# A vision tower on one Trainium2 core: the last group's experts summed in SBUF, and another order for row sums, image statistics and factors

## The chip, the cores and the metric

The kernel runs on one core of one Trainium2 chip, as one program. A core has TensorE (PE, matrix products), VectorE (DVE), ScalarE (ACT), GpSimd (POOL) and SyncE (SP, which here only issues transfers), each with its own instruction stream; they meet at semaphores. The metric is the time of one execution on the device in microseconds (us). The profile is of one other execution; its times are counted from the start of its span.

## What is computed

64 images of 2 x 104 x 104 become 128 channels by 170 tokens each (169 patches of 8 x 8 and a class token). There is one layer, in three stages:

```python
# token stage: the image and four diagonal shifts of it by 4 pixels, one layernorm per image, a patch convolution
concat = jnp.concatenate((x, lu, ru, ld, rd), axis=1)
mean = jnp.mean(concat, axis=(1, 2, 3), keepdims=True); var = jnp.var(concat, axis=(1, 2, 3), keepdims=True)
normed = (concat - mean) * jax.lax.rsqrt(var + EPS) * gamma[None] + beta[None]
y = conv(normed, W, stride 8) + b ; h = concat([cls_tok, tokens])
# graph stage: layernorm over channels, a two-layer graph convolution over the 128 channels, a projection
h = h + graph(_layernorm(h))
# attention and experts: causal attention in 2 heads with normalised q and k, then 8 experts, all of them for every token
gate = softmax(y @ gate_W + gate_b)
hid = gelu(einsum('bnd,edf->bnef', y, W1) + b1)
eo = einsum('bnef,efd->bned', hid, W2) + b2
h = h + einsum('bned,bne->bnd', eo, gate)
```

The mean and variance of an image need sums over all its pixels, of which the four shifted copies lose a rim.

## The kernel before

**Tiling.** The result tile `ht` is 128 channels by 64 x 170 tokens, f32. The expert layer works on groups of 4 images (`T` = 680 columns, halves of `TH` = 340, 16 groups). Each group's 8 experts have 4 chunks of 128 hidden rows each, in all 32 slots. In slot s PE forms hidden rows s (`of_o`, L1059), ScalarE applies the gelu (L667, and for most slots a half-precision copy, L672), DVE forms the difference part (L1537) and for eight slots the copy (L1535), and three slots later PE multiplies both with the second weights (`experts_out`, L1094). After every fourth slot DVE's `weigh` (L1550) takes the two halves of an expert's sum out of PSUM, adds the bias and multiplies by the gate row, into one of two `tmp` tiles. GpSimd adds that tile to the output in DRAM by an accumulating transfer (L498), eight per group, each after the one before it has landed; SP has stored the group's base, `ht` without the experts, by a plain transfer (L405). The gate rows go to a scratch in DRAM and come back spread over the partitions in three transfers (L398).

**Preamble.** The token stage runs over 65 points (13 rows of patches by 5 shifts). At each, DVE multiplies a row by gamma (`gammas`, L1347) and PE convolves (L816). Beside the points an order written out by hand says what else each engine does at which point: for the first group its graph stage and queries and keys (`GRAPH_0`, `QK_0`), for the second its first layernorm (`FIRST_1`), the folding of the first weights with the attention's output matrix (`FOLD_PE` products L783, `FOLD_HI` copies on ScalarE, `FOLD_LO` differences on DVE, `first_lo`, L1463), and 20 further points (`LATE`, 65 to 84) with no convolution. `kn` (L1420) scales the keys and waits for PE's cast of the roots (L857).

**Image statistics.** Images 0 to 7 are summed at the start. For images 8 to 63 accumulating transfers add rows into `sums4` while the token stage runs. `sums_rest` (L1277 to L1295, three parts) reduces these on DVE, at points 62, 63 and 64 in `DVE_SUMS`; `image_stats` (L825) is one product on PE; `image_moments` (L1302 to L1306) and `image_factors` (L1313 to L1325, twelve dependent operations of 128x56) are on DVE. The factors are first used by `fix` (L1371, L1374) from slot 6 of the first group's expert stage on.

**First attention.** After the late points DVE takes the row maxima of the scores in two parts (L1428, L1431), ScalarE the exponentials (L633), DVE normalises (L1436, L1443), PE turns the probabilities (L995) and weighs the values (L1007). In between PE does products of the second group's graph stage (L829) into another PSUM pair. The scores of part 1 use the PSUM pair in which the folds and the statistics' product are.

## Time and profile before

| | us |
|---|---|
| timed runs, median (lowest to highest) | 1461.5 (1458.69 to 1461.71) |
| profiled execution, own time | 1459.82 |
| its span | 1457.8 |
| PE busy | 1415.5 (97%) |
| DVE busy | 1215.5 (83%) |
| ScalarE busy | 1106.4 (76%) |
| GpSimd busy | 290.9 (20%) |

A timeline row gives the start, the length, the engine, the line, the operation with tiles and shapes, how many of them, and in brackets how long the engine was idle in front and what released it. Rows of several instructions can overlap a little with the next one, so the distance between two starts is the better price. Most tiles are parts of one SBUF tensor and appear as `area`; `pair` is PSUM. The granted TensorE clock (PEclk) is a share of 2.4 GHz: 1.00 is 2.4 GHz, 0.50 is 1.2 GHz.

### The profile page before, as it was taken

The page shows a single profiled execution, that of the slowest core. Times are in us where ns is not written, and L with a number is a line of the kernel's source. Part 1 is how long each engine was busy: PE and PEld are TensorE (multiplying, and loading weights), DVE is VectorE, ACT ScalarE, POOL GpSimd, SP SyncE. Part 2 cuts the span into 40 slices and gives each one's busy share as a digit, 9 for nine tenths or more (in the row PEclk, how much of TensorE's full clock was granted, in tenths as well). Part 3 has the DMA queues.
Part 4 walks back from the last instruction along what each step waited for, and adds up shares of the span by engine and source line. Part 5 has one row for each costly group of instructions (what it writes and reads, how often), then busy time and mean ns, then how long its engine had stood idle before and what let it go on. Part 6 is the DMA issues. An engine that isn't in the chain of part 4 may idle for free.

```text
span 1457.8 us, 31164 instructions
## 1 busy us (share of the span) xinstructions
PE 1415.5 (97%) x10945; PEld 982.8 (67%) x10945; DVE 1215.5 (83%) x2576; ACT 1106.4 (76%) x1880; POOL 290.9 (20%) x293
## 2 busy tenths in 40 slices
PE   8998899999999999999999999999999999999997
PEld 5665667676676677676676677676676767676665
DVE  7886898888888888889788888889888888887765
ACT  5343678787878888887878878888878878878766
POOL 2124032131301212131301212131301112130101
PEclk9999999999999999999999999999999999999999
DMA  8796232434333332424233332424342332424334
GB/s 263 180 237 128 105 61 30 121 43 109 45 107 46 80 73 29 124 38 114 39 108 45 93 60 29 124 38 115 40 113 38 100 53 33 120 38 116 49 99 57
DMA packets 40771, 125.54 MB, mean 86 GB/s; under 512 B 5792, under 2 KB 6048, under 8 KB 38560
## 3 DMA queue, kind: packets, MB, share of 16 engines
q0 software_dynamic: 22464, 55.81, 26.3%
q1 hardware_dynamic: 18128, 69.28, 13.2%
q8 instruction: 19, 0.31, 0.1%
q14 instruction: 16, 0.13, 0.0%
q10 hardware_dynamic: 144, 0.01, 0.0%
HBM read 68.98 MB, written 50.48 MB: 82 GB/s over the span
## 4 chain that ended last, share of the span: by engine, by line
PE 74%; DVE 10%; DMA 7%; issue 5%; ACT 2%; DVEq 0%; POOL 0%; SPq 0%; POOLq 0%; ACTq 0%
PE pair L1094 25%; PE pair L1059 22%; PE pair L829 9%; PE pair L816 4%; DMA area<-gate_scratch 3%; DVE area L1537 3%; PE pair L1007 3%; PE pair L924 2%; PE pair L980 2%; PE pair L995 2%; DMA area<-area 2%; PE pair L955 1%; DVE area L1550 1%; DMA gate_scratch<-gt_t 1%; ACT area L672 1%
## 5 line engine op out<-in xcount | busy, mean ns | idle before, releaser
L667 ACT ACTIVATE area<-pair,pack_b_sb 128x680 f32<-128x680 f32 x512 | 423.5, 827 | 180.6 <-PE pair L1059 180.5
L1537 DVE TENSOR_TENSOR area<-area 128x680 f16<-128x680 f32 x512 | 454.0, 892 | 110.1 <-ACT area L672 104.1
L1059 PE MATMUL pair<-area,ws 128*128 128x340 f16 x3072 | 530.7, 308 | 5.5 <-ACT area L667 2.8
L1094 PE MATMUL pair<-area,ws 128*128 128x340 f16 x3072 | 526.8, 307 | 6.9 <-DVE area L1550 3.8
L1094 PEld LDWEIGHTS pair<-area,ws 128*128 128x128 f16 x3072 | 290.2, 98 | 160.6 <-DVE area L1550 26.4
L1059 PEld LDWEIGHTS pair<-area,ws 128*128 128x128 f16 x3072 | 292.4, 97 | 155.0 <-ACT area L667 8.3
L672 ACT ACTIVATE area<-pair,pack_b_sb 128x680 f16<-128x680 f32 x384 | 316.2, 824 | 0.0
L498 POOL DMA_DIRECT2D tower_out<-area x128 | 114.2, 892 | 997.3 <-DVE area L1550 943.4
L1550 DVE SCALAR_TENSOR_TENSOR area<-pair,pack_b_sb,area 128x340 f32<-128x340 f32 x256 | 133.9, 565 | 10.2 <-PE pair L1094 8.5
L633 ACT ACTIVATE area<-pair,nbias,root 85x85 f32<-85x85 f32 (+1 forms) x256 | 112.5, 466 | 0.2
L455 POOL TENSOR_TENSOR area<-area 128x680 f16<-128x680 f32 x56 | 89.2, 1601 | 45.3 <-ACT area L596 43.0
L596 ACT ACTIVATE area<-pair,pack_b_sb 128x680 f32<-128x680 f32 x92 | 81.9, 936 | 4.4 <-PE pair L829 3.8
L1535 DVE CAST area<-area 128x680 f16<-128x680 f32 x128 | 67.0, 524 | 12.2 <-ACT area L667 5.7
L816 PE MATMUL pair<-area,pack_a_sb 128*128 128x336 f32 (+1 forms) x164 | 56.1, 484 | 4.4 <-DVE area L1347 3.5
L1443 DVE TENSOR_SCALAR area<-area,rs 85x85 f32<-85x85 f32 (+1 forms) x256 | 56.4, 281 | 2.3
L633 ACT ACTIVATION_READ_ACCUMULATOR area<-pair,nbias,root 85x1 f32 x256 | 54.9, 214 | 0.0
L641 ACT ACTIVATE area<-pair,att_b 128x340 f16<-128x340 f32 x32 | 17.3, 540 | 40.7 <-PE pair L1007 40.7
L816 PEld LDWEIGHTS pair<-area,pack_a_sb 128*128 128x128 f32 x164 | 30.9, 195 | 24.5 <-DVE area L1347 5.6
L571 ACT ACTIVATE ht<-pair 128x392 f32<-128x392 f32 (+1 forms) x26 | 19.8, 871 | 34.9 <-PE pair L816 34.9
L1450 DVE COPY area<-pair 85x510 f32<-85x510 f32 x64 | 43.4, 678 | 2.3 <-PE pair L995 0.4
L995 PE MATMUL pair<-ident,area 85*85 85x85 f32 x384 | 41.9, 246 | 3.1 <-DVE area L1467 2.4
L924 PEld LDWEIGHTS pair<-head_m,area 128*85 128x85 f32 x512 | 43.5, 156 | 1.9
(238 smaller groups left out, 1758.5 us busy)
## 6 DMA issues: line engine op xcount, KB each, us to landing
tower_out<-area POOLq DMA_DIRECT2D x128, 340.0 KB, 4.7
area<-gate_scratch SPq DMA_DIRECT2D x16, 1360.0 KB, 9.9
area<-gate_scratch SPq DMA_DIRECT2D x16, 1020.0 KB, 7.1
area<-cells SPq DMA_DIRECT2D x16, 392.0 KB, 8.7
area<-cells POOLq DMA_DIRECT2D x14, 392.0 KB, 6.5
area<-area POOLq DMA_DIRECT2D x14, 392.0 KB, 6.3
tower_out<-ht SPq DMA_DIRECT2D x16, 340.0 KB, 2.3
area<-gate_scratch SPq DMA_DIRECT2D x16, 340.0 KB, 4.4
```

The lines of the kernel that those rows point to most:

```text
L455: pool.tensor_tensor(h1_l[:, half], relu[c], h1_h[:, half], ALU.subtract).then_inc(relu_lo, 1)
L498: pool.dma_start(out[:, g * T:(g + 1) * T], tmp[e % 2], accum_op=ALU.add).then_inc(out_done, 16)
L596: last = nc.scalar.activation(two(part), halves(ps), ACT.Relu, bias=scal[:, 4 + c:5 + c], scale=scal[:, c:c + 1])
L633: nc.scalar.activation(probs[:, b * SCORE + o0:b * SCORE + o0 + w], score_ps_at(b)[:, h, c * QC:c * QC + w], ACT.Exp, bias=nbias[:, n:n + ...
L667: nc.scalar.activation(two(hid[slot % NHID]), halves(hid_ps[slot % 2]), ACT.Gelu_apprx_tanh, bias=col(COL_B1 + slot)).then_inc(hid_ready, 1)
L672: nc.scalar.activation(two(hh[slot % NPART]), halves(hid_ps[slot % 2]), ACT.Gelu_apprx_tanh, bias=col(COL_B1 + slot)).then_inc(hhi_act, 1)
L816: last = mm(cells_ps(p, j), conv_w[:, shift * D:(shift + 1) * D], xg[n % XG][:, c0 * BZ:c1 * BZ], start=(shift == 0), stop=(shift == SHIFT ...
L829: last = mm(ps[:, j, 0:TH], lhs, rhs[:, j, :], start=start, stop=stop)
L1059: last = mm(hid_ps[slot % 2][:, j, 0:TH], lhs[:, w], rhs[:, j * TH:(j + 1) * TH], start=(i == 0), stop=(i == 2))
L1094: last = mm(eo_ps[:, j, 0:TH], lhs[:, w], rhs[:, j * TH:(j + 1) * TH], start=(m % CH == 0 and i == 0), stop=(m % CH == CH - 1 and i == 2))
L1537: v.tensor_tensor(hl[slot % NPART], hid[slot % NHID], hh[slot % NPART], ALU.subtract).then_inc(hlo_ready, 1)
L1550: v.scalar_tensor_tensor(tmp[e % 2][:, j * TH:(j + 1) * TH], eo_ps[:, j, 0:TH], b2_s[:, e:e + 1], gbc[:, e * T + j * TH:e * T + (j + 1) * ...
```

## The change

Three things. In the last group there is no base store and no accumulating transfer: DVE's `weigh` adds each weighted half to `ht` in SBUF, and SP stores the two halves when the eighth expert has been added. The row sums move behind the last gamma, to points 66 to 68, and `kn` and three of the fold's differences move forward. The statistics' product goes behind the scores of the first attention, into the second half of the pair `eo_ps`; the moments go between the two parts of the maxima, and the factors behind the second part, out of slot 4 of the first expert stage.

```diff
-        "cast": 62, "kn": 73}
+        "cast": 62, "kn": 65}
-DVE_SUMS = {62: 0, 63: 1, 64: 2}
+DVE_SUMS = {66: 0, 67: 1, 68: 2}
-IMG_SLOT = 4
-FOLD_LO = {0: 36, 1: 36, 2: 42, 3: 46, 4: 64, 5: 69, 6: 77, 7: 77}
+FOLD_LO = {0: 36, 1: 36, 2: 42, 3: 46, 4: 64, 5: 65, 6: 69, 7: 70}
...
+            def last_store():
+                for j in range(2):
+                    half = slice((G - 1) * T + j * TH, (G - 1) * T + (j + 1) * TH)
+                    sp.wait_ge(part_added, 2 * (E - 1) + j + 1)
+                    sp.dma_start(out[:, half], ht[:, half]).then_inc(last_out, 16)
             for g in range(G):
-                base(g)
+                if g < G - 1:
+                    base(g)
...
-            for g in range(G):
+            for g in range(G - 1):
                 weigh(g, later=g > 0, ahead=g < G - 2)      # GpSimd
...
-                if b == 0 and not later:
-                    pe.wait_ge(tok_done, 2 * NP)
+                if b == 2 and not later:
+                    pe.wait_ge(img_step[1], 3)              # PE, values
...
                 elif m == 1:
-                    pe.wait_ge(img_step[1], 3)
+                    pe.wait_ge(fold_lo, E)                  # PE, scores
...
                     for m in range(NB // 2):
                         scores(g, m, later)
+                    pe.wait_ge(tok_done, 2 * NP)
+                    image_stats(1, BZ, eo_ps[:, 1, 0:2 * BZ])
...
-            pe.wait_ge(fold_lo, E)
-            image_stats(1, BZ, hid_ps[1][:, 1, 0:2 * BZ])
...
-                    for m in range(NB // 2):
-                        maxima(g, m)
+                    maxima(g, 0)
+                    image_moments(1, BZ, eo_ps[:, 1, 0:2 * BZ])
+                    maxima(g, 1)
+                    image_factors(1, BZ, BA)
...
-                if e >= 2 or later:
+                if (e >= 2 or later) and not (last and e >= 2):
                     dve.wait_ge(out_done, 16 * (g * E + e - 1))
...
+                if last:
+                    for j, done in enumerate((half_ready, tmp_ready)):
+                        dve.wait_ge(done, g * E + e + 1)
+                        if e:
+                            dve.wait_ge(part_added, 2 * (e - 1) + j + 1)
+                        acc = ht[:, g * T + j * TH:g * T + (j + 1) * TH]
+                        v.tensor_tensor(acc, acc, tmp[e % 2][:, j * TH:(j + 1) * TH], ALU.add).then_inc(part_added, 1)
...
-                    if not later and slot == IMG_SLOT:
-                        image_factors(1, BZ, BA)
```

## Rows read from the trace of the kernel before

**Rows 1.** Timeline of DVE, 130 to 151 us, its rows explained above.

```profile
132.73 0.39 DVE L1277 TENSOR_TENSOR statz<-area 128x224 f32<-128x224 f32 x1 [9.27 <-DMA area<-area]
...
134.86 0.91 DVE L1347 TENSOR_TENSOR area<-area,pack_a_sb 128x728 f32<-128x728 f32 x1
135.69 0.85 DVE L1283 TENSOR_TENSOR area<-area 128x672 f32<-128x672 f32 x1
...
137.61 0.91 DVE L1347 TENSOR_TENSOR area<-area,pack_a_sb 128x728 f32<-128x728 f32 x1
...
139.04 0.27 DVE L1291 SCALAR_TENSOR_TENSOR statz<-statz 128x112 f32<-128x112 f32 x1
...
139.84 0.68 DVE L1463 TENSOR_TENSOR ws<-pair,ws 128x512 f16<-128x512 f32 x1
140.44 0.85 DVE L1420 TENSOR_TENSOR area<-area,pair 128x680 f32<-128x680 f32 x1
...
144.02 0.22 DVE L1302 COPY statz<-pair 128x56 f32<-128x56 f32 x1 [0.57 <-PE pair L825]
...
145.49 1.28 DVE L1428 TENSOR_REDUCE mx<-pair 85x4 f32<-85x340 f32 x2 [0.75 <-PE pair L984]
...
146.95 1.28 DVE L1428 TENSOR_REDUCE mx<-pair 85x4 f32<-85x340 f32 x2
...
150.25 0.17 DVE L1436 RECIPROCAL rs<-sm 85x4 f32<-85x4 f32 x1 [1.82 <-ACT area L633]
```

**Rows 2.** Timeline of PE, 131 to 146 us.

```profile
131.58 0.75 PE L857 MATMUL pair<-ident,area 85*128 85x85 f32 x8
135.83 4.55 PE L816 MATMUL pair<-area,pack_a_sb 128*128 128x392 f32 x8 [3.50 <-DVE area L1347]
...
145.38 1.12 PE L980 MATMUL pair<-area 64*85 64x85 f32 x16
```

**Rows 3.** Timeline of all engines, 169 to 198 us.

```profile
169.87 1.29 SPq L398 DMA_DIRECT2D area<-gate_scratch  x3
...
172.14 0.18 DVE L1313 TENSOR_SCALAR statz<-statz 128x56 f32<-128x56 f32 x1
...
175.10 0.92 DVE L1407 SCALAR_TENSOR_TENSOR area<-area,pack_b_sb,pair 128x680 f32<-128x680 f32 x1
...
177.53 1.32 PE L829 MATMUL pair<-area,wqk_h 128*128 128x340 f16 x4 [3.00 <-DVE area L1413]
...
178.17 1.04 DVE L1550 SCALAR_TENSOR_TENSOR area<-pair,pack_b_sb,area 128x340 f32<-128x340 f32 x2
...
197.87 1.08 PE L1094 MATMUL pair<-area,ws 128*128 128x340 f16 x6 [0.96 <-DVE area L1550]
```

**Rows 4.** Windows between gate reductions: length, each engine's busy time, PEclk, DMA share, GB/s.

```profile
162.76:249.33 86.57, 82.14 (x664) 57.40 (x663) 77.37 (x163) 66.33 (x113) 25.73 (x23) 0.98 0.37 82
249.33:331.07 81.74, 80.89 (x664) 56.77 (x663) 69.97 (x151) 66.31 (x113) 16.59 (x15) 1.00 0.35 73
```

The busy times stand in the order PE, PE's weight loads, DVE, ScalarE, GpSimd.

**Rows 5.** Windows around two falls of the granted clock, same columns.

```profile
1378.50:1381.80 3.30, 1.51 (x19) 1.26 (x17) 3.26 (x11) 3.30 (x16) 0.54 (x1) 0.98 0.72 93
1381.80:1392.00 10.20, 9.94 (x68) 7.34 (x68) 4.95 (x16) 3.79 (x10) 0.00 (x0) 0.50 0.03 6
...
177.50:180.30 2.80, 2.77 (x11) 1.52 (x12) 2.79 (x5) 0.85 (x2) 0.79 (x1) 0.52 0.95 399
```

**Rows 6.** Window in the last group's expert stage, same columns.

```profile
1411.00:1446.00 35.00, 35.00 (x245) 23.54 (x244) 24.55 (x36) 27.70 (x37) 4.63 (x5) 1.00 0.38 51
```

**Rows 7.** The end: timeline, SP's final wait, and the page's transfers (KB, us to landing).

```profile
1449.77 1.05 DVE L1550 SCALAR_TENSOR_TENSOR area<-pair,pack_b_sb,area 128x340 f32<-128x340 f32 x2 [0.70 <-PE pair L1094]
...
L414 SPq EVENT_SEMAPHORE  x1: 17/17/17, 1456.9 to 1456.9; - x1
...
tower_out<-area POOLq DMA_DIRECT2D x128, 340.0 KB, 4.7
...
tower_out<-ht SPq DMA_DIRECT2D x16, 340.0 KB, 2.3
area<-gate_scratch SPq DMA_DIRECT2D x16, 340.0 KB, 4.4
```

More of the change, by code:

```diff
@@ L297, in vit_tower @@
         half_used, half_ready, base_done, out_done = map(sem, ("half_used", "half_ready", "base_done", "out_done"))
+        part_added, last_out = map(sem, ("part_added", "last_out"))
         PREP_PE, PREP_ACT, PREP_DVE = 9, 8, 22
@@ L412, in _ @@
                         second_weights(e)
-            sp.wait_ge(base_done, 16 * G)
-            sp.wait_ge(out_done, 16 * E * G)
+            last_store()
+            sp.wait_ge(base_done, 16 * (G - 1))
+            sp.wait_ge(out_done, 16 * E * (G - 1))
+            sp.wait_ge(last_out, 32)
         @block.gpsimd
@@ L1537, in experts, with weigh @@
                 v.tensor_tensor(hl[slot % NPART], hid[slot % NHID], hh[slot % NPART], ALU.subtract).then_inc(hlo_ready, 1)
-            def weigh(g, e, later):
+            def weigh(g, e, later, last=False):
                 dve.wait_ge(half_used, g * E + e + 1)
@@ L1551, in weigh, with expert_slot @@
                                            gbc[:, e * T + j * TH:e * T + (j + 1) * TH], ALU.add, ALU.mult).then_inc(done, 1)
-            def expert_slot(g, slot, later):
+                if last:
[5 more added lines that the diff above has]
+                        v.tensor_tensor(acc, acc, tmp[e % 2][:, j * TH:(j + 1) * TH], ALU.add).then_inc(part_added, 1)
+            def expert_slot(g, slot, later, last=False):
                 if slot >= LAG and (slot - LAG) % CH == CH - 1:
-                    weigh(g, (slot - LAG) // CH, later)
+                    weigh(g, (slot - LAG) // CH, later, last)
                 if slot < SLOTS:
@@ L1562, in ffn @@
                 for slot in range(SLOTS + LAG):
-                    expert_slot(g, slot, later)
-                    if not later and slot == IMG_SLOT:
-                        image_factors(1, BZ, BA)
+                    expert_slot(g, slot, later, last=not successor)
                     if successor and 0 <= slot - SLOTS < NB // 2:
@@ L1603, in _ @@
                     prepare(DVE_PREP[n])
+            for n in LATE:
                 if n in DVE_SUMS:
                     sums_rest(DVE_SUMS[n])
-            for n in LATE:
                 chain(n)
-            image_moments(1, BZ, hid_ps[1][:, 1, 0:2 * BZ])
             attention(0, False, True)
```

## The prediction

> **What bounds the kernel now.** I read the waits of 100 to 200 us first, because three of the four edits lie there, then the timelines of VectorE (DVE) and TensorE (PE) through that stretch, then windows over one pass of the experts' loop, and last the final 35 us. The kernel is one long preamble (token stage, first group's attention), then 15 more groups that repeat, then a tail.
>
> In the preamble the reader should see one hole. At point 62 of the token stage DVE stands at the image row sums, which wait for the accumulating transfers: idle 9.27 us, until 132.73 [rows 1]. Two multiplications by gamma (points 63 and 64, L1347 at 134.86 and 137.61) are behind it on DVE, so PE, which starts the cast of the roots at 131.58 and is through at 132.3, idles 3.50 us and ends its last convolutions at 140.4 [rows 1, 2]. After that DVE is the engine that everything follows, until it starts the first normalisation at 150.25, which waited 1.82 us for ScalarE's exponentials; these waited for the maxima (1.28 for a pair of reductions at 145.49 and at 146.95) [rows 1].
>
> In the first group's expert stage DVE has no gap from 168 on. The image factors (L1313 to L1325) stand in it from 172.14 to 175.10; behind them is the chain xh, its half-precision parts, which PE awaits for 3.00 us before the queries at 177.53 [rows 3]. The first such pass, from one gate reduction to the next, takes 86.57 us, a later one 81.74 with PE busy for 80.89 of it: later groups are bound by PE, and the diff touches none of them but the last [rows 4].
>
> At the end PE has finished and the time is a transfer: the last two products (L1550) end at 1450.82, the accumulating store takes 4.7 us from its issue and lands at 1456.9, 0.9 before the span's end [rows 7]. It is issued only at about 1452.2 (1456.9 - 4.7), since it waits for its predecessor.
>
> **Part A, row sums and moments.** After the change gammas 63 and 64 run at 123.5, when DVE used to go idle. PE's order is unchanged, it is busy until 132.3, and then both convolutions are ready. They end at least the 3.50 us of that wait earlier, and as the second also stood for its gamma (137.61 + 0.91), near 134.8 in place of 140.4: 5.6 is the upper bound of this part. But DVE now sets the pace. From 132.3 it does: kn (L1420, moved from 73 to 65), 0.8, and first_lo 5, 0.6 (start to start 139.84 to 140.44), to 133.7; here the sums start 1.0 later than before. Row sums part 0 without the gamma, 132.73 to 134.86, 2.1; part 1, 135.69 to 137.61, 1.9; part 2, 139.04 to 139.84, 0.8; first_lo 6 and 7, 1.2: DVE is at 139.8. The second scores now wait for fold_lo, so the first maxima, 139.8 to 141.2 (1.46 from one pair to the next), run beside the second scores, which take no longer than that; the statistics' product and its latency 0.6 (the wait at 144.02), moments, three operations at 0.25 (the twelve of the factors took 2.96), 0.7: 142.5; second maxima 1.4, 143.9; factors 2.96, 146.9. ScalarE has had its first bias since 141.2; before, it took 3.3 us from the bias (146.95) to the first normalisation (150.25), table load included, so it is ready at 144.5 and has 2.4 in hand: no wait remains there [rows 1, 3]. Normalise starts at 146.9 against 150.25: 3.4 us. From there both versions run the same DVE list. Ends: -1.0 (sums later, nothing else gained) and 5.6; I take 3.4, the sum of DVE's own rows.
>
> What is behind the added waits: PE now holds scores 1 for fold_lo, and behind it plain, values and the second group's graph products. By the same sums (my estimates) it idles 2.0 us, from 137.8 to 139.8, and again about 2.3, from 146.2 to 148.5, when the first values are copied out. The work there has slack, as DVE is late, if the clock holds (below). ScalarE is free of it.
>
> **Part B, factors out of the expert stage.** They took 175.10 - 172.14 = 2.96 us of a DVE without gaps, and PE's 3.00 us wait ends with the same chain [rows 3]. With them gone hx's parts end at 174.5, just as PE arrives. The granted clock after the old wait was 0.52 for 2.8 us [rows 5], so PE also saves up to 1.4 there; but PE meets DVE again at 197.87 (a wait of 0.96 for L1550), where only DVE's gain counts. Late next would be the gate row for the first expert: issued at 169.87, 4.4 to land, 174.3, while DVE needs it at 178.17 - 2.96 = 175.2 [rows 3, 7]. It stays hidden by 0.9. Ends: 2.1 (that transfer late by twice its margin) and 4.83 (86.57 - 81.74, the whole excess of the first pass) [rows 4]; I take 3.0.
>
> **Part C, last group.** Removed: one plain store of the base (hidden at 1331.8), 8 accumulating stores on GpSimd, waits for them. Added on DVE: 16 additions of 128x340 f32. A tensor_tensor of 672 columns took 0.85 and one of 224 took 0.39 [rows 1], so 340 take 0.51, 0.43 from start to start. All but the last two lie beside PE's work. In 35 us of that group, five experts, DVE is busy 24.55 and PE 35.00 [rows 6]: an expert leaves DVE 2.1 us free, its two additions take 0.9. Queued behind them is the next difference part (L1537), which PE needs only three slots later. So I cost them at nothing; were that cover gone, the sixteen would cost 6.9. The last two are on the path: 1450.8 + 0.43 + 0.51 = 1451.75. The first half's store is issued at 1451.4, the second's at 1451.8. A plain store of 340 KB took 2.3 us to land [rows 7]; a half has no row and lies between 1.2 (half of that) and 2.3 plus 1 for the other half in its way. I take 2.1, near the whole one, as both are in flight together. Landing 1453.9 against 1456.9: 3.0. Ends: 1.8 and 3.9.
>
> The Trainium skill speaks against splitting the store: its page "DMA: Bandwidth & Descriptors", section "Anatomy of one DMA — SWDGE (gpsimd) path", puts about 2.0 us of fixed cost on each transfer and only the bytes over 436 GB/s on top, and its rules advise coalescing. By it the last half takes 2.4 and one whole store behind the second addition 2.8, so the split would still save 0.4, and part C would be 2.7. The trace is below that formula: a whole store of 340 KB took 2.3, not 2.8 [rows 7]; no run here shows a half.
>
> **Sum.** 3.4 + 3.0 + 3.0 = 9.4. The profiled execution took 1459.8 (span 1457.8): 1450.4. The median of the three timed runs is 1461.5, 1.7 above it, which would give 1452.1; I name 1451.0, between the two. The ends of all three parts together would be 1456.9 and 1445.5; I don't expect them at once.
>
> **Rivals.**
> 1. The clock falls in the first attention. In the last group's attention PE was busy 1.51 of 3.30 us, and then the granted clock was 0.50 (1.2 GHz) for 10.2 us; after the 3.00 us wait before 177.53 it was 0.52 for 2.8 us [rows 3, 5]. The new waits of 2.0 and 2.3 us are between those cases. If it falls at 148.5, graph 2, two turns and two weighings and graph 3 double: some 4.5 us more, less 0.7 of slack: about 4, time 1455. 20%.
> 2. More returns in the first expert stage: PE's gain of 4.4 isn't stopped at 197.87 because the splits on GpSimd meet DVE at another place. 1.4 more: 1449.6. 12%.
> 3. The additions are not hidden: with 32 waits of DVE on itself and its own lateness, difference parts come late and PE waits 6.9 in the last group: 1457.9, no measurable change. Against it: the slack above. 4%.
> 4. Slower than before: the clock falls already at 137.8 and stays down through all of the first attention, which is nearly continuous PE work from the second scores at 145.4 to the gate reduction at 162.76 (17.4 us) [rows 2, 4]. At 1.2 GHz that is up to 17.4 more, less 4.3 of waits that it fills: 13, time 1464. It decides from 9.4 us of path work at the lower clock. For it: the 10.2 us row. Against: here products of 340 columns stand between the small ones, and behind such work the clock was back after 2.8 us. 3%.
> 5. The reordering of A gains nothing because another wait, not seen, holds DVE at the old time: 1454.4. 5%.
> The forecast has the rest, 56%.
>
> **Numbers.** About 0.2% (2.9 us) is what a measurement of this kernel can tell from no change. The range 1447.5 to 1455.8 holds the forecast with its ends, rival 2, 5 and most of 1. Faster by more than 0.2% are the forecast and rivals 1, 2 and 5, 93%; a little of that I leave for the spread of the runs. Slower is rival 4; rival 3 and the spread are no change.
>
> **What would show it.** Right: L1347's last two before 126, L1277 at about 133.6 with a wait only on PE's cast in front, L816 ending near 135, L1436 first at 147; L1407 right behind L1537 at slot 4 with no PE wait over 0.5 before the queries; a pass of 83 to 84 us; 16 DVE additions in the last group with PE still 35 of 35 busy; the last landing 3 us behind the last product. Wrong: a granted clock of 0.5 between 137 and 160; PE waits for L1537 after 1404; a half store of 3 us or more.

## The result, and the profile after

| | before | after |
|---|---|---|
| timed runs, median (lowest to highest) | 1461.71 (1458.69 to 1463.63), 5 runs | 1451.83 (1449.51 to 1456.65), 5 runs |
| profiled execution, own time | 1459.82 | 1456.65 |
| its span | 1457.8 | 1454.9 |

The ratio is 0.9937 (95% interval 0.9918 to 0.9955): 9.9 us less by the medians, where 10.5 was forecast against 1461.5. The profiled execution of after is the slowest of its five; it shows the first rival at work.

Line numbers after the insertions are up to 13 higher: gamma is L1356, `conv` L825, the row sums L1286 on, the moments L1311 on, the factors L1322 to L1334, the maxima L1437, normalise L1445, the difference part L1548, `weigh` L1561, the new additions L1569, the last stores L411.

The timeline of DVE, 120 to 152 us, answers to [rows 1]:

```profile
123.78 5.58 DVE L1356 TENSOR_TENSOR area<-area,pack_a_sb 128x728 f32<-128x728 f32 x4
...
134.42 0.86 DVE L1429 TENSOR_TENSOR area<-area,pair 128x680 f32<-128x680 f32 x1 [3.80 <-PE pair L866]
...
135.80 0.38 DVE L1286 TENSOR_TENSOR statz<-area 128x224 f32<-128x224 f32 x1
...
142.10 1.27 DVE L1437 TENSOR_REDUCE mx<-pair 85x4 f32<-85x340 f32 x2
...
144.02 0.22 DVE L1311 COPY statz<-pair 128x56 f32<-128x56 f32 x1 [0.45 <-PE pair L834]
...
148.73 0.22 DVE L1334 SCALAR_TENSOR_TENSOR img<-statz,img 128x56 f32<-128x56 f32 x1
148.99 0.17 DVE L1445 RECIPROCAL rs<-sm 85x4 f32<-85x4 f32 x1
```

The wait for the accumulating transfers is gone; DVE waits for PE's cast instead. The gammas are through when it comes, the sums stand behind `kn`, and from 134.42 to the first normalisation DVE has one wait of 0.45. The last four gammas took 5.58 us, 1.4 each, where two took 1.73 in the kernel before; GpSimd was at work on the folds beside them from 124.96 to 131. They end at 129.36, or 127.3 in before's time, where the forecast wanted them before 126; in front of a wait of 3.80 that costs nothing. That GpSimd slows them is likely (its cast beside them took 1.83, one of the same shape at 131.01 without them 0.61), but no run tests it. PE in the same stretch [rows 2]:

```profile
133.63 0.75 PE L866 MATMUL pair<-ident,area 85*128 85x85 f32 x8
134.22 2.65 PE L825 MATMUL pair<-area,pack_a_sb 128*128 128x392 f32 x8
...
142.24 1.12 PE L989 MATMUL pair<-area 64*85 64x85 f32 x16 [2.19 <-DVE ws L1472]
...
147.17 1.36 PE L838 MATMUL pair<-area,gcn_m 128*128 128x340 f32 x4
150.81 0.66 PE L1004 MATMUL pair<-ident,area 85*85 85x85 f32 x6 [2.27 <-DVE area L1476]
```

The last eight convolution products take 2.65 without a wait, where they had 3.50 of wait and 4.55. So the old wait had a fall of the clock behind it too: the granted clock was 0.59 from 136 to 140 in before's trace and is 1.00 there in after's. The two new waits are there, 2.19 and 2.27. Windows, with the columns of [rows 4]: first the stretch behind the second wait, then the first pass of the experts from gate reduction to gate reduction, then the window of [rows 6], moved by nothing:

```profile
152.00:163.00 11.00, 11.00 (x65) 8.32 (x63) 6.21 (x17) 2.10 (x4) 0.00 (x0) 0.50 0.00 1
167.28:250.78 83.50, 81.08 (x664) 56.77 (x663) 74.99 (x152) 66.28 (x113) 25.88 (x23) 1.00 0.37 85
1411.00:1446.00 35.00, 35.00 (x245) 23.59 (x243) 28.24 (x46) 27.63 (x36) 0.00 (x0) 1.00 0.00 1
```

The granted clock is 0.50 (1.2 GHz) for all of 152 to 163: PE is busy without a gap and gets half as much done. The pass is 83.50 against 86.57. In the last group PE is full and GpSimd empty, and DVE has 3.7 more in 35 us. PE in the first pass, and the end (timeline, the DMA view, SP's final wait), answer to [rows 3, 7]:

```profile
199.31 1.08 PE L1105 MATMUL pair<-area,ws 128*128 128x340 f16 x6 [1.71 <-DVE area L1561]
```

```profile
1450.55 1.05 DVE L1561 SCALAR_TENSOR_TENSOR area<-pair,pack_b_sb,area 128x340 f32<-128x340 f32 x2 [0.70 <-PE pair L1105]
1451.51 0.93 DVE L1569 TENSOR_TENSOR ht<-ht,area 128x340 f32<-128x340 f32 x2
1452.04 0.81 SPq L411 DMA_DIRECT2D tower_out<-ht  x2
...
tower_out<-ht SPq DMA_DIRECT2D x2, 170.0 KB, 1.9
...
SPq L423 <- DMA tower_out<-ht: 1.5, 1, 1.5
```

From the end of the last `weigh` (1450.55 + 1.05 = 1451.60) to the end of the span are 3.30; before they were 6.98 (1457.8 - 1450.82).

**Where the 2.9 us between the two profiled executions went.** I cut both traces at the same events and compare the pieces; with this table the experiments are read too. The columns: A, from the start of PE's cast of the roots to the first normalisation; att, from there to the first gate reduction; B, from the first gate reduction to the second; last, from the 16th gate reduction to the last `weigh`'s end; C, from there to the span's end; conv, the start of PE's next products behind the first convolution's 32 products, near 20 us. The stretch between the second and the 16th gate reduction is left out. Clock is the mean granted clock of the whole execution.

| kernel | conv | A | att | B | last | C | span | clock |
|---|---|---|---|---|---|---|---|---|
| before | 20.30 | 18.67 | 12.51 | 86.57 | 58.45 | 6.98 | 1457.8 | 0.993 |
| after | 22.36 | 15.36 | 18.29 | 83.50 | 58.05 | 3.30 | 1454.9 | 0.991 |
| again | 22.35 | 16.75 | 13.73 | 83.51 | 58.05 | 3.26 | 1451.4 | 0.993 |
| fill | 24.40 | 17.02 | 12.34 | 83.11 | 58.05 | 3.3 | 1452.2 | 0.995 |
| graph2 | 22.12 | 15.36 | 13.96 | 83.51 | 58.10 | 3.2 | 1450.0 | 0.995 |
| late | 20.84 | 13.80 | 16.32 | 86.14 | 58.09 | 3.25 | 1451.5 | 0.993 |
| fill2 | 22.30 | 15.35 | 12.34 | 83.89 | 57.60 | 3.3 | 1448.9 | 0.995 |
| tail | 20.43 | 18.94 | 12.51 | 86.96 | 58.57 | 3.28 | 1454.5 | 0.994 |
| sums62 | 23.84 | 21.21 | 12.34 | 83.56 | 58.06 | 3.26 | 1455.2 | 0.995 |
| adds2_whole | 22.46 | 15.35 | 13.67 | 83.62 | 58.99 | 3.60 | 1450.8 | 0.995 |
| slot4 | 21.90 | 13.22 | 12.50 | 87.35 | 58.07 | 3.2 | 1449.9 | 0.995 |
| fill_last | 22.32 | 15.36 | 12.35 | 83.90 | 58.38 | 3.26 | 1446.6 | 0.998 |
| fill_all | 21.66 | 15.36 | 12.35 | 82.77 | 58.60 | 3.22 | 1445.8 | 1.000 |

Before to after: A -3.31, B -3.07, C -3.68, together -10.06. Against that stand +2.06 before 22 us, where the diff changes nothing, and +5.78 in the first attention; both are stretches at a lower granted clock. The rest is -0.3 in the middle and -0.4 in the last group.

### The profile page after: what moved, and what is told of

It is laid out like the page before. It is cut to its first block, busy times and chain, and to the rows that moved or that the text cites. A ratio compares the mean times of both kernels' runs of the same rounds, so it can differ in the third digit from the quotient of the medians.

```text
span 1454.9 us, 31173 instructions
## 1 busy us (share of the span) xinstructions
PE 1419.2 (98%) x10945; PEld 986.4 (68%) x10945; DVE 1223.4 (84%) x2592; ACT 1105.7 (76%) x1880; POOL 284.9 (20%) x285
## 4 chain that ended last, share of the span: by engine, by line
PE 75%; DVE 12%; issue 6%; DMA 5%; ACT 2%; DVEq 0%; SPq 0%; ACTq 0%; POOLq 0%
PE pair L1105 25%; PE pair L1070 22%; PE pair L838 9%; PE pair L825 4%; DVE area L1548 3%; PE pair L1016 3%; DMA area<-gate_scratch 2%; PE pair L1004 2%; PE pair L933 2%; PE pair L989 2%; DVE area L1561 1%; DMA area<-area 1%; PE pair L964 1%; ACT area L681 1%; DMA gate_scratch<-gt_t 1%
## 5 line engine op out<-in xcount | busy, mean ns | idle before, releaser
L1548 DVE TENSOR_TENSOR area<-area 128x680 f16<-128x680 f32 x512 | 454.1, 892 | 104.9 <-ACT area L681 99.1
L507 POOL DMA_DIRECT2D tower_out<-area x120 | 106.8, 890 | 925.3 <-DVE area L1561 909.5
L1561 DVE SCALAR_TENSOR_TENSOR area<-pair,pack_b_sb,area 128x340 f32<-128x340 f32 x256 | 133.9, 565 | 9.8 <-PE pair L1105 8.6
L825 PE MATMUL pair<-area,pack_a_sb 128*128 128x336 f32 (+1 forms) x164 | 54.2, 473 | 0.9 <-ACT ht L580 0.9
L1004 PEld LDWEIGHTS pair<-ident,area 85*85 85x85 f32 x384 | 39.4, 163 | 11.6 <-DVE area L1452 8.1
L825 PEld LDWEIGHTS pair<-area,pack_a_sb 128*128 128x128 f32 x164 | 30.3, 190 | 19.6 <-issue 2.0
```

The costliest lines, as they stand in the source:

```text
L507: pool.dma_start(out[:, g * T:(g + 1) * T], tmp[e % 2], accum_op=ALU.add).then_inc(out_done, 16)
L825: last = mm(cells_ps(p, j), conv_w[:, shift * D:(shift + 1) * D], xg[n % XG][:, c0 * BZ:c1 * BZ], start=(shift == 0), stop=(shift == SHIFT ...
L1004: last = tr(eo_ps[0:QC, b % 2, n * QC:(n + 1) * QC], probs[:, b * SCORE + n * QC:b * SCORE + (n + 1) * QC], ident[0:QC, 0:QC])
L1548: v.tensor_tensor(hl[slot % NPART], hid[slot % NHID], hh[slot % NPART], ALU.subtract).then_inc(hlo_ready, 1)
L1561: v.scalar_tensor_tensor(tmp[e % 2][:, j * TH:(j + 1) * TH], eo_ps[:, j, 0:TH], b2_s[:, e:e + 1], gbc[:, e * T + j * TH:e * T + (j + 1) * ...
```

## The experiments

The theory: the three parts bring what their terms say, and what an execution of the changed kernel loses again is the granted clock, which falls behind PE's new waits in some executions. The rival for the 5.78: a new wait of PE or DVE that costs time by itself. Each part has a test of its own besides.

### again: the changed kernel once more

No edit.

> The changed kernel unaltered, five more times. Theory C (clock): its times fall into two kinds. Where the granted clock does not fall in the first attention 1449 to 1452; where it falls after the 2.3 us wait in front of the first turn of probabilities, 1455 to 1457, and then the span has a mean clock lower by about 0.003 or more. Rival W (order): the first attention is longer because of the new waits themselves, in every execution, and the times scatter around 1452 without two kinds.

1451.85 (1449.55 to 1456.11, 6 runs), ratio 0.9937 (0.9921 to 0.9953). The parts repeat to 0.04 us in B and C. The clock doesn't. Windows of this execution:

```profile
138.00:142.00 4.00, 1.83 (x19) 0.98 (x18) 3.83 (x10) 0.74 (x2) 0.00 (x0) 0.99 0.00 0
142.00:146.00 4.00, 3.98 (x27) 3.07 (x28) 2.06 (x7) 2.54 (x7) 0.00 (x0) 0.59 0.02 4
146.00:150.00 4.00, 3.84 (x34) 2.65 (x32) 3.59 (x15) 4.00 (x21) 0.00 (x0) 1.00 0.00 0
150.00:154.00 4.00, 2.02 (x9) 1.59 (x10) 3.90 (x15) 3.34 (x12) 0.00 (x0) 0.77 0.00 0
154.00:158.00 4.00, 4.00 (x32) 3.05 (x31) 2.97 (x13) 0.23 (x1) 0.00 (x0) 0.81 0.00 0
158.00:162.00 4.00, 4.00 (x41) 3.17 (x40) 2.75 (x5) 0.86 (x2) 0.00 (x0) 1.00 0.01 2
```

It fell twice, once behind each new wait (2.19 at 142.02, 2.15 at 151.98), each time for some 3 to 4 us: A is 1.39 longer than after's and att 1.39 longer than the 12.34 of undisturbed executions. In the profile of after it fell behind the second wait alone, and for 13 us. So one kernel has several courses through this stretch: A and att together took 33.65 in after's trace and 30.48 in this one, against 27.69 with both waits filled (fill2, below).

The two kinds of times that were expected did not come: the six spread over the whole range. Nor does the mean clock put them in order. 1456.11 has a mean clock of 0.994, as 1452.19 has, and among the five runs of after 1455.39 has 0.994, as 1451.83 has. The fall accounts for the 5.78 of the profiled execution (0.991), but these two slow ones are some 4 us above others of the same clock. The kernel before has such executions too (1465.83 and 1459.58, both at 0.993). What makes them is open; no trace was taken of one.

### fill: products in the second wait

26 products of 128x170 in half precision, into a part of PSUM that nobody reads until it is overwritten, ahead of the first turn. The output is unchanged.

```diff
+                if not later:
+                    for _ in range(26):
+                        mm(fr_ps[:, 0, TH:TH + 170], wv_h[:, :], xh_h[:, 0:170], start=False, stop=False)
```

> 26 extra products of 128x170 f16 (some 1.9 us of TensorE work whose result nobody reads) stand in the wait in front of the first turn of probabilities. Theory C: the granted clock stays at 1.00 from 150 to 163 us, the first attention is as short as forecast (first normalisation to gate reduction about 12.5 us, against 18.3 in the profile of the changed kernel), all five times are 1449 to 1452. Rival W: the extra work sits in front of the turns and helps nothing: normalisation to gate reduction stays near 18, times 1452 to 1457.

1450.98 (1448.66 to 1453.96, 5 runs), ratio 0.9924 (0.991 to 0.9938). The second wait is filled, the clock stays at 1.00 behind it, and att is 12.34. The times reach beyond the 1449 to 1452 that were expected: the profiled execution is the slowest of the five, with 2.0 more than after's in conv and 1.66 more in A. The first wait stayed open, and in this execution it cost:

```profile
144.41 1.94 PE L989 MATMUL pair<-area 64*85 64x85 f32 x16 [2.52 <-DVE ws L1475]
```

Sixteen products that take 1.12 at full clock took 1.94, and DVE then waited 1.77 for the statistics' product behind them. That is the part of the theory I had not priced: the first wait has its own fall, worth 1.4 to 1.7 in A.

### graph2: useful work in the second wait

The second group's graph product 2 is issued ahead of the first turn, not behind it.

```diff
+                if not later:
+                    graph_of(2)
...
-                graph_of(2)
+                if later:
+                    graph_of(2)
```

> The second group's graph product 2 moves in front of the first turn of probabilities in the first attention, so the wait there shrinks from 2.3 to about 1.1 us with no work added. Theory C: no fall of the clock, normalisation to gate reduction about 12.5 us or 0.3 less, times 1449 to 1451. Rival W: no change from the changed kernel.

1452.69 (1450.23 to 1454.22, 5 runs), ratio 0.9941 (0.9926 to 0.9955): no gain. The wait of 2.3 became three shorter ones, and the clock fell behind the third:

```profile
150.59 0.66 PE L1004 MATMUL pair<-ident,area 85*85 85x85 f32 x6 [1.14 <-DVE area L1479]
152.18 0.66 PE L1004 MATMUL pair<-ident,area 85*85 85x85 f32 x6 [0.93 <-DVE area L1479]
153.67 0.68 PE L1004 MATMUL pair<-ident,area 85*85 85x85 f32 x6 [0.25 <-DVE area L1455]
...
154.00:158.00 4.00, 4.00 (x21) 2.74 (x20) 2.27 (x8) 0.54 (x1) 0.00 (x0) 0.58 0.01 2
```

The work borrowed from between the turns filled one hole by opening others. What held the clock in these runs was extra products (fill2) or the wait gone (slot4).

### late: the factors behind the second part of the first attention's output

```diff
-                    image_factors(1, BZ, BA)
...
+                if not later:
+                    image_factors(1, BZ, BA)
```

> The factors (2.96 us on VectorE) move from in front of the first normalisation to behind the second o_lo of the first attention, in front of dev2. Theory C: normalisation starts 2.4 us earlier, when ScalarE is ready, TensorE's wait in front of the first turn is near 0, no fall of the clock; 2.0 of the 2.4 are given back before dev2, where VectorE idled 0.95: about 0.4 faster than a changed kernel without the fall, 1449 to 1451. Rival W: the factors are as costly there, the times stay as in the changed kernel, 1452 to 1456.

1452.90 (1449.0 to 1457.57, 6 runs), ratio 0.9944 (0.9925 to 0.9962): not better. Normalise came 1.56 earlier than after's (13.80 against 15.36), although the clock had fallen in front of it. But att is 3.98 above the undisturbed 12.34, and B is 2.6 above after's. 2.96 of the first is the factors again, now in front of the gate reduction; the other 1.0 includes the end of the first fall (the clock is 0.72 from 146 to 148) and was not taken apart:

```profile
158.31 0.18 DVE L1322 TENSOR_SCALAR statz<-statz 128x56 f32<-128x56 f32 x1
...
161.46 0.86 DVE L1410 TENSOR_TENSOR area<-ht,pair 128x680 f32<-128x680 f32 x1 [0.24 <-DVE img L1334]
```

The second is the clock: PE now waits behind them, 1.48 for the gate stage's ScalarE row (it is busy for 1.53 of the 3.00 us from 160 to 163), and the granted clock is 0.50 from 165 to 171.

```profile
163.18 1.57 PE L850 MATMUL pair<-mean_m,area 128*85 128x1 f32 x16 [1.48 <-ACT area L612]
...
165.00:167.00 2.00, 1.94 (x7) 1.04 (x8) 1.86 (x6) 1.61 (x5) 0.00 (x0) 0.50 0.00 0
167.00:169.00 2.00, 2.00 (x8) 0.90 (x6) 0.07 (x1) 1.52 (x2) 0.00 (x0) 0.50 0.00 0
```

The factors' 2.96 are on the path in both places, and each place opens a hole of PE's of its own.

### fill2: both new waits filled

Fill's products, and 26 of the same ahead of the second scores.

```diff
+                        if m == 0:
+                            for i in range(26):
+                                mm(fr_ps[:, 0, TH:TH + 170], wv_h[:, :], xh_h[:, 0:170], start=(i == 0), stop=(i == 25))
```

> The changed kernel with products that nobody reads (26 of 128x170 f16, some 1.9 us) in both waits of TensorE in the first attention: between the scores of part 0 and part 1, and in front of the first turn. Theory C (the waits let the clock fall, now in the one, now in the other): clock 1.00 from 133 to 166 us, cast of the roots to first normalisation 15.4 us, from there to the gate reduction 12.4, median 1 to 3 us below the changed kernel's 1451.8, with only the scatter of the first 20 us left (up to 4 us). Rival W (the clock is set by something other than these waits): falls as in the changed kernel, the same median.

1450.45 (1449.46 to 1450.83, 5 runs), ratio 0.9918 (0.9905 to 0.9931). The clock is 1.00 from 134 to 162:

```profile
142.18 1.12 PE L989 MATMUL pair<-area 64*85 64x85 f32 x16 [0.28 <-DVE ws L1478]
...
150.76 0.66 PE L1004 MATMUL pair<-ident,area 85*85 85x85 f32 x6 [0.37 <-DVE area L1482]
```

A is 15.35 and att 12.34. Both releasers are as late as before the filling (142.18 against 142.24, 150.76 against 150.81), so the waits by themselves cost nothing; this rules the rival out. The runs also lie closer, with a standard deviation of 0.48 us against 2.14 in again. That is five runs against six, and fill_last, below, has the same fillings and 2.12, by one execution of 1452.69; so the closer times are no proof that the fillings remove the spread. The median is 1.4 lower; the intervals of the two ratios overlap, so the gain on the median is likely and not shown, while the loss in single executions (5.8 in after's) is shown in the traces.

### tail: part C alone on the kernel before

The last group's additions and stores, and nothing of the order of sums, moments and factors. The lines shown are the additions; the base store and the accumulating transfers of the last group go too, as in the change.

```diff
+                if last:
+                    for j, done in enumerate((half_ready, tmp_ready)):
+                        dve.wait_ge(done, g * E + e + 1)
+                        if e:
+                            dve.wait_ge(part_added, 2 * (e - 1) + j + 1)
+                        acc = ht[:, g * T + j * TH:g * T + (j + 1) * TH]
+                        v.tensor_tensor(acc, acc, tmp[e % 2][:, j * TH:(j + 1) * TH], ALU.add).then_inc(part_added, 1)
```

> Only part C on the kernel before: the last group's experts summed in SBUF, two plain stores. Theory: everything up to the last weighing as before, from the gate reduction of the last group to the last weighing 58.1 to 58.5 us, last weighing to the end of the span 3.3 in place of 7.0: 3.7 faster, 1457.5 against 1461.2. Rival (additions on the path): 58.45 grows by several us and the gain is under 1.

1458.38 (1455.21 to 1460.88, 12 runs), ratio 0.9973 (0.9964 to 0.9982), 3.6 below before's 1461.97 of the same session. C is 3.28 against 6.98, so 3.70; A, att and B are before's within 0.4. Part C stands alone and is worth about 3.7.

### sums62: the row sums back at points 62 to 64

Row sums ahead of the last gammas again; the rest of the change kept.

```diff
-DVE_SUMS = {66: 0, 67: 1, 68: 2}
+DVE_SUMS = {62: 0, 63: 1, 64: 2}
```

> The changed kernel with the row sums back at points 62 to 64, in front of the last two gammas; all else as changed. Theory: VectorE idles again some 9 us for the accumulating transfers, TensorE 3.5 in front of the last convolutions; both gammas (1.7) and their convolutions and the folds behind them come after, so the first normalisation is 2 to 4 us later than in the changed kernel (cast of the roots to normalisation 17.5 to 19.5 against 15.4). Rival: the row sums were not the bound there, within 1 us of the changed kernel.

1455.04 (1451.8 to 1457.01, 6 runs), ratio 0.9946 (0.9933 to 0.996): 3.2 above the changed kernel by the medians, 4.6 above fill2. PE's wait for the gamma is back, and the second gamma with it:

```profile
139.78 2.04 PE L825 MATMUL pair<-area,pack_a_sb 128*128 128x392 f32 x4 [3.92 <-DVE area L1356]
142.53 2.79 PE L825 MATMUL pair<-area,pack_a_sb 128*128 128x392 f32 x4 [0.71 <-DVE area L1356]
```

and DVE waits for the folds, as these wait for PE:

```profile
147.69 0.69 DVE L1472 TENSOR_TENSOR ws<-pair,ws 128x512 f16<-128x512 f32 x1 [2.45 <-ACT ws L656]
...
149.65 1.28 DVE L1437 TENSOR_REDUCE mx<-pair 85x4 f32<-85x340 f32 x2
```

A is 21.21 against 15.36, 5.85 longer, where 2 to 4 were expected (17.5 to 19.5). The rest is the clock: PE was at 0.50 from about 140.6 to 147.4, the four products of 142.53 took 2.79 in place of 1.3, and the four of the folds behind them 3.03 in place of 1.88. The first two of the folds are what DVE's wait of 2.45 ends with, so the clock makes up some 2.3 of the 5.85 (my estimate from these rows), and 3.5 are left for the order. Against before, A is 2.54 longer: 1.90 behind the first maxima, where factors and moments now stand (6.66 against 4.76 [rows 1]), and 0.64 in front of them. In A and B together sums62 is only 0.47 below before, and after 6.38. So the new order of the row sums is what pays for the factors' new place.

### adds2_whole: twice the additions, one whole store

For the first seven experts of the last group each addition is done twice (the second into a tile that nobody reads), and the group is stored by one transfer behind the last addition. DVE also waits for each expert's spare additions before the next expert's.

```diff
-                for j in range(2):
-                    half = slice((G - 1) * T + j * TH, (G - 1) * T + (j + 1) * TH)
-                    sp.wait_ge(part_added, 2 * (E - 1) + j + 1)
-                    sp.dma_start(out[:, half], ht[:, half]).then_inc(last_out, 16)
+                whole = slice((G - 1) * T, G * T)
+                sp.wait_ge(part_added, 2 * E)
+                sp.dma_start(out[:, whole], ht[:, whole]).then_inc(last_out, 16)
...
+                    if e < E - 1:
+                        for j in range(2):
+                            v.tensor_tensor(xh[:, j * TH:(j + 1) * TH], dev[:, j * TH:(j + 1) * TH],
+                                            tmp[e % 2][:, j * TH:(j + 1) * TH], ALU.add).then_inc(spare, 1)
```

> Two edits in the last group, each with its own interval in the trace. (1) For experts 0 to 6 each addition is done twice, the second into a scratch tile: 1.7 us of VectorE per expert against a free 2.1. Theory: hidden, gate reduction to last weighing stays 58.1 (within 0.3). Rival: already the change's additions ate the cover, then it grows by up to 6. (2) One store of 340 KB behind both additions in place of two halves: lands 0.3 to 0.5 later than the second half did, last weighing to end of the span 3.7 against 3.3; by the Trainium skill's formula (2.0 us plus bytes over 436 GB/s, page DMA: Bandwidth & Descriptors) 0.4 later.

1452.59, one run. The window of [rows 6] and the one wait of PE in it:

```profile
1411.00:1446.00 35.00, 34.23 (x238) 22.84 (x237) 31.79 (x55) 26.50 (x34) 0.00 (x0) 1.00 0.00 1
...
1444.64 1.91 PE L1104 MATMUL pair<-area,ws 128*128 128x340 f16 x12 [0.77 <-DVE area L1547]
```

DVE is busy 31.79 of 35 and PE loses 0.77 once; last grows by 0.94. The fourteen more additions are 6.5 us of DVE time and cost 0.94. The wait is more than the 0.3 that was expected, far less than the rival's 6. So the sixteen of the change are hidden, with room for nearly as many again. The whole store ends 0.30 later than the two halves (3.60 against 3.30).

### slot4: part A without the factors in front of the normalisation

Fill2's first filling, the factors back in slot 4 of the first expert stage.

```diff
-                    image_factors(1, BZ, BA)
...
+                    if not later and slot == 4:
+                        image_factors(1, BZ, BA)
```

> As the kernel with both waits filled (1450.5), but the factors back in slot 4 of the first expert stage, and the second filling left out, since that wait goes with them. It prices the move of the factors by itself, with the clock held in the first attention. Theory: normalisation starts as soon as ScalarE is ready (13.0 us after the cast of the roots, not 15.4), and the first pass of the experts takes 86.5 in place of 83.5 to 83.9, with TensorE's 3 us wait and the clock at half behind it: net 0.6 slower, about 1451. Rival (parts A and B add up as forecast, 3 us for the factors): 3 slower, 1453.5.

1451.71 (1450.84 to 1452.46, 5 runs), ratio 0.9929 (0.9917 to 0.9942). Normalise is 2.13 earlier than fill2's and now waits for ScalarE; the wait before the queries is back at its old size:

```profile
146.01 0.17 DVE L1450 RECIPROCAL rs<-sm 85x4 f32<-85x4 f32 x1 [0.73 <-ACT area L642]
...
173.28 0.76 PE L838 MATMUL pair<-area,wqk_h 128*128 128x340 f16 x4 [3.00 <-DVE area L1427]
```

B is 87.35 against 83.89: 2.13 gained, 3.46 lost. Moving the factors is worth 1.3 us by itself, by the pieces (A and B together 100.57 against 99.24) and by the medians (1451.71 - 1450.45), though the intervals of these two overlap. The two terms A and B of the forecast are not independent: without the factors in it A is 5.45 (18.67 - 13.22), and B then nothing (87.35 against before's 86.57).

### fill_last: the clock of the last attention held

Fill2, and 43 such products at five places of the last group's attention, where the clock fell in the kernel before [rows 5].

```diff
+                def spare(n):
+                    if not ahead:
+                        for _ in range(n):
+                            mm(fr_ps[:, 0, TH:TH + 170], wv_h[:, :], xh_h[:, 0:170], start=True, stop=True)
```

> As the kernel with both waits filled (1450.5), and 43 more such products in the waits of the last group's attention, where TensorE runs at half clock for some 10 us in every profile so far. Theory C: the clock stays at 1.00 there, from the last maxima to the gate reduction about 17.5 us in place of 20.9, 1447.1 by the median. Rival: VectorE sets the pace of that attention anyway, under 1 us.

1447.65 (1446.18 to 1452.69, 6 runs), ratio 0.9907 (0.9892 to 0.9922), 2.8 below fill2; the intervals of the two overlap a little, so it is the traces that show the gain. A window of 20 us over that attention, first before, then fill_last (where the attention ends at 1384.96 and the experts' stage follows); and the last maxima and the gate reduction in fill2 and in fill_last:

```profile
1376.00:1396.00 20.00, 16.26 (x128) 11.67 (x126) 14.00 (x43) 12.97 (x42) 0.93 (x1) 0.74 0.13 18
```

```profile
1376.00:1396.00 20.00, 18.26 (x172) 13.08 (x169) 14.13 (x36) 14.91 (x30) 0.00 (x0) 1.00 0.21 43
```

```profile
1371.03 1.28 DVE L1443 TENSOR_REDUCE mx<-pair 85x4 f32<-85x340 f32 x2 [0.84 <-PE pair L993]
1388.03 0.29 DVE L1509 TENSOR_REDUCE lg<-pair 85x64 f32<-85x128 f32 x1 [1.74 <-PE pair L1069]
```

```profile
1370.81 1.28 DVE L1453 TENSOR_REDUCE mx<-pair 85x4 f32<-85x340 f32 x2 [0.83 <-PE pair L993]
1384.96 0.29 DVE L1519 TENSOR_REDUCE lg<-pair 85x64 f32<-85x128 f32 x1 [1.13 <-PE pair L1079]
```

From the last pair of maxima to the gate reduction it is 14.15 at a mean clock of 1.00 against 17.00 at 0.70: 2.85 us, where 3.4 were expected, and the fillings are the only difference. The old kernel had this loss too (1392.37 - 1375.36 = 17.01, clock 0.70). One of the six runs was 1452.69 at a mean clock of 0.999, 4 us above the others. Its excess can't be the clock; it is of the kind seen in again, and open.

### fill_all: also the wait of the first convolution

Fill_last, and eight products of 128x128 in f32 in PE's wait near 10 us, behind which the first convolution's clock fell in most traces.

```diff
+                    if shift == 1:
+                        for _ in range(8):
+                            mm(hid_ps[0][:, 0, 0:D], conv_w[:, 0:D], conv_w[:, 0:D], start=True, stop=True)
```

> The same, and 8 f32 products of 128x128 in TensorE's wait of 1.1 to 2.1 us at 10 us, behind which the 32 products of the first convolution took 9.3 us in three profiles and 11.0 to 12.3 in five. Theory C: always 9.3, so 1.5 us below the kernel before it, about 1445.6, and a spread under 1 us. Rival: that clock is the start-up of the chip, not this wait: no change, or up to 1 us slower.

1447.66 (1447.28 to 1449.59, 4 runs), ratio 0.9907 (0.9892 to 0.9921). The clock was held everywhere (mean 1.000) and the 32 products took 9.26 in place of 11.02, yet the median is fill_last's, where 2 us less were expected:

```profile
10.29 2.44 PE L802 MATMUL pair<-pack_a_sb 128*128 128x128 f32 x16
12.57 9.26 PE L808 MATMUL pair<-ws,pack_a_sb 128*128 128x416 f32 x32
```

The filling ends near 12.6, about 1 us after the convolution could have started (11.50 in after). It gives back 1.1 of the 1.8 that it saves. A shorter one wasn't run.

Fill_last and fill_all are the fastest kernels of this study, by their medians some 4 us below the changed kernel and 14 below before's.

## Why the prediction was right

**Part A, 3.4: right in size and in course.** Measured 3.31. Two of the forecast's instants hold to 0.1 when one takes off the 2.06 by which this execution started later, and those between them to 0.3: L1286 at 135.80 - 2.06 = 133.7 (forecast 133.7), normalise at 148.99 - 2.06 = 146.93 (146.9). The sum of DVE's own rows was the right price and the 5.6 of PE's waits only its upper end. Both added waits were foreseen at 2.0 and 2.3; they are 2.19 and 2.27.

**Part B, 3.0: right.** 86.57 to 83.50 is 3.07. The PE wait of 3.00 before the queries is gone, and PE then meets DVE at L1561, 1.71 in place of 0.96, so DVE's gain and not PE's counts, as costed. Rival 2 (1.4 more) did not come in any trace; the shortest B is 82.77, 0.73 less. The two parts hang together, though: slot4 shows that moving the factors takes 3.46 out of B and puts 2.13 into A, and 1.3 is what the move brings.

**Part C, 3.0: the mechanism right, a term too small.** It is 3.68, and 3.70 in tail. The forecast comes to 4.0 from the last `weigh`'s end to the span's end, and 3.30 were measured: 0.85 for the additions up to the second store's issue at 1452.45 (forecast 1.0), 1.9 to land (2.1), and 0.55 behind the landing (0.9). The last is the largest miss: I had carried before's remainder over without asking what it consists of. The additions cost nothing, as costed: PE is busy for 35.00 of 35 us beside them, and last is 58.05 against 58.45 before and 58.57 in tail. That refutes rival 3, and by adds2_whole nearly twice their number costs 0.94.

By the pages I had cited: the Trainium skill, page "DMA: Bandwidth & Descriptors", section "Anatomy of one DMA — SWDGE (gpsimd) path", has a fit of 2.0 us plus the bytes over 436 GB/s for transfers issued by GpSimd, from which I had worked out 2.4 and 2.8 as estimates for 170 and 340 KB. These stores are issued by SP and took 1.9 and 2.3, 0.5 less each, so only the difference per byte agrees. The split does pay: 0.30 by adds2_whole, where the page's figures made it 0.4.

**Rival 1, given 20% at 1455: it happens in part of the executions.** The forecast treated the clock as a case that comes or doesn't come for the kernel. It comes execution by execution: in the profiled one of after it cost 5.8 (I had said 4), in again twice 1.4, in fill2 nothing. One of my signs of being wrong, a granted clock of 0.5 between 137 and 160, is there in after's trace. The median of 1451.83 probably has some of it in (fill2's is 1.4 lower, which is not clear of noise). After's highest run, 1456.65, is outside my range by this fall and by the 2.06 of the first 22 us together; without either it would lie inside. Rival 4 priced the fall of the first wait with the whole attention behind it; it does occur (again, late), but the clock is back after 4 to 7 us. Rival 5 fell with the measured 3.31.

**Why the sum was near.** That 1451.0 was met within 0.9 is in part luck. The parts bring 10.06 against 9.4, by C, which I had 0.7 too small. The middle and the last group bring 0.7 that I had not counted. From before's median of 1461.71 that would give 1451.0; the falls of the clock, which were not in the central case, would then have taken back about 0.9 at the median (an estimate). And I had set the forecast 1.1 below the 1452.1 that the median of before less 9.4 gives, without a mechanism for it. These misses cancel.

**What stays open.** Why the same wait is followed by a fall in one execution and not in another. What makes some executions 4 us slower at the same mean clock. And the first 20 us: the 32 products of the first convolution took 9.33 in before's trace, behind a wait of 1.31, and 11.02 in after's, behind 2.14, at a granted clock of 0.59 from 11.5 to 14 and 0.66 from 14 to 16. The wait is for a product with gamma on DVE, which in after's trace waits for a transfer. Its length does not decide alone: 1.08 in graph2 had 11.02 behind it, 1.58 in late had 9.33. Both traces of kernels without the new order (before, tail) show the short form and eight of the eleven others 22.0 or more in the table. Nothing in the diff acts there, and late has 20.84, so I take it for chance; that the change brings it is not ruled out.

## What to carry to other kernels

When a change moves waits to another engine, price the wait's time and the clock behind it separately: a wait of 2.2 us among small products cost nothing in itself here and up to 5.8 us through the clock. Read such a stretch in several executions before believing one. The spread of the times alone doesn't tell: here it had a second source that the mean clock does not show. A long DVE sequence costs its full length wherever DVE has no gap: ask what moving it is worth by itself (here 1.3), not what disappears from the old place (3.0).

## What the runs showed of the hardware

- The loss lasts while PE has no idle time: in after the clock stayed at 0.50 (1.2 GHz) through 11.00 us in which PE was busy for 11.00, doing turns, small products and graph products.
- Products whose results nobody reads paid for themselves: with 52 in the first attention the clock was 1.00 from 134 to 162 and att 12.34 in place of 18.29 and 13.73, and 43 in the last one brought 2.85 us.
- The same wait in the same kernel had different sequels: behind the first one (2.19) the clock stayed at 1.00 in after and fell for some 4 us in again; behind the second (2.27 and 2.15) it fell for 13 us in after and for some 4 in again, and behind one of 2.28 in sums62 not at all.
- Useful work moved into a wait did not hold the clock (graph2): waits of 0.93 to 1.14 between the next small products stood in its place, and it fell behind them. A wait of 1.48 (late) had a fall behind it too.
- Additions of 128x340 in f32 took 505 ns each, 0.43 from start to start (a pair is 0.93), as the forecast had interpolated from 672 and 224 columns.
